# The last five batches' norms go into the rounds, the loop of rounds is written out, and idle products stand ahead of the first transposes

## What is computed

```
xn = layernorm(x)                       # (x - mean) / sqrt(var + eps), no weights
s  = mamba(xn)                          # W_in, causal convolution, silu, delta, scan over the tokens, W_out
g  = silu(ffn(xn))                      # (silu(xn wg) * (xn wu)) wd
x  = x + s * g
```

## Time and profile before

| what | value |
|---|---|
| median of 3 runs | 764.2 us (763.67 to 766.95) |
| the profiled execution: own time, span | 764.31 us, 762.5 us |
| busy: TensorE, VectorE, ScalarE, GpSimd | 660.6, 651.2, 495.9, 492.1 us |
| scans, line 1678 | 128 instructions, 288.5 us |
| first scan starts | 334.20 us |
| mean granted TensorE clock | 0.974 |

### The profile page before, as it was taken

One profiled execution on the slowest core, in us unless ns is written; L12 is line 12 of the kernel. 1 busy time (PEld: TensorE's weight loads), 2 busy tenths in 40 slices (PEclk: granted clock), 3 DMA queues, 4 the chain that ended last, 5 costly groups with the idle time before them and its releaser, 6 DMA issues. The chain is left out here.

```text
span 762.5 us, 13530 instructions
## 1 busy us (share of the span) xinstructions
PE 660.6 (87%) x3984; PEld 486.1 (64%) x3984; DVE 651.2 (85%) x1124; ACT 495.9 (65%) x1002; POOL 492.1 (65%) x306
## 2 busy tenths in 40 slices
PE   0898999999899964779998998998998999988785
PEld 0875556556555542347776886777787777767665
DVE  4968877777566646899999999899999999999998
ACT  0565666666444434778779778677787787797453
POOL 1002663000054545058899999999999999999995
PEclk9999999999999995989999999999999999999999
DMA  7900110001222218525515535335237156065000
GB/s 176 313 1 11 39 38 24 0 0 28 62 71 67 64 49 101 152 84 166 138 48 150 123 100 125 98 112 138 68 112 179 31 157 161 17 176 129 1 13 16
DMA packets 43223, 67.48 MB, mean 88 GB/s; under 512 B 6297, under 2 KB 30369, under 8 KB 43169
## 3 DMA queue, kind: packets, MB, share of 16 engines
q1 hardware_dynamic: 31888, 48.42, 20.7%
q0 software_dynamic: 9552, 17.85, 11.5%
q10 hardware_dynamic: 1728, 0.57, 0.5%
HBM read 46.08 MB, written 9.74 MB: 73 GB/s over the span
## 5 line engine op out<-in xcount | busy, mean ns | idle before, releaser
L1678 DVE TENSOR_TENSOR_SCAN xnT_all<-psum,nfT_all 128x1024 f32<-128x1024 f32 x128 | 288.5, 2277 | 0.0
L1258 PEld LDWEIGHTS psum<-W_out,xnT_all 128*128 128x128 f32 x2048 | 235.7, 192 | 60.2 <-issue 37.9
L1258 PE MATMUL psum<-W_out,xnT_all 128*128 128x128 f32 x2048 | 241.7, 276 | 31.6 <-DVE acc L1694 29.4
L1423 ACT ACTIVATE psum<-delta,A 128x511 f32<-128x511 f32 x256 | 165.0, 682 | 72.5 <-DVE xnT_all L1678 72.4
L1238 POOL TENSOR_TENSOR nfT_all<-nf_rows,du 128x1024 f32<-128x1024 f32 x63 | 147.2, 2361 | 30.9 <-DVE nfT_all L1760 29.8
L1238 POOL TENSOR_TENSOR nfT_all<-attn_all,du 128x1024 f32<-128x1024 f32 x64 | 157.5, 2605 | 0.0
L570 POOL DMA_INDIRECT moe_dram<-xnT_all x40 | 38.8, 969 | 121.1 <-ACT xnT_all L826 121.1
L1694 DVE SCALAR_TENSOR_TENSOR acc<-psum,Cc,acc 128x128 f32<-128x128 f32 x284 | 78.2, 340 | 6.2 <-PE psum L1258 6.0
L559 POOL DMA_INDIRECT xs_dram<-nf_rows,pos x32 | 33.6, 1050 | 74.7 <-DVE pos L880 55.8
L1258 PE MATMUL psum<-vo_all,W_taps 128*128 (+4 forms) x128 | 60.2, 618 | 3.0 <-DVE vo_all L1790 2.3
L1460 ACT ACTIVATE ts<-psum,Cc 128x128 f32<-128x128 f32 x188 | 52.8, 360 | 4.1 <-PE psum L1258 4.1
(11 more groups left out here) (215 smaller groups left out, 1111.6 us busy)
## 6 DMA issues: line engine op xcount, KB each, us to landing
nf_rows<-bt_dram SPq DMA_DIRECT2D x32, 512.0 KB, 4.7
attn_all<-bt_dram SPq DMA_DIRECT2D x32, 512.0 KB, 4.1
delta<-rl POOLq DMA_DIRECT2D x7, 512.0 KB, 6.9
e<-ab POOLq DMA_DIRECT2D x7, 512.0 KB, 5.8
delta<-e POOLq DMA_DIRECT2D x7, 512.0 KB, 6.3
xs_dram<-attn_all SPq DMA_DIRECT2D x4, 645.0 KB, 8.6
xnT_all<-xs_dram SPq DMA_DIRECT2D x40, 64.5 KB
x_all<-in_x_dram SPq DMA_DIRECT2D x8, 256.0 KB, 6.0
```

Of the source, the lines that this page charges most:

```text
L1258: return nc.tensor.matmul(o, l, r, start=start, stop=stop)
L1423: ins = nc.scalar.activation(dA[:, i % RA, k, 1:L], delta[:, p, h, 1:L], ACT.Exp, scale=A[:, h, 2 * q + k:2 * q + k + 1])
L1678: nc.vector.tensor_tensor_scan(hring[:, i % R, :, :].rearrange("p n l -> p (n l)"), dA[:, i % RA, :, :].rearrange("p n l -> p (n l)"), dbx ...
```

## The change

- `KEEP_WARM = 13` products (`ident` with 512 columns of `xn1T_all`, into bank 3, which nothing reads) stand on TensorE ahead of `turn(0)`. They wait for nothing.
- Batches 3 to 7 are no longer normed by VectorE. `shifts(2)` makes their reciprocals and `nb1 = -mean * reciprocal`, and ScalarE norms batch b + 3 in round b at q = 4 (`norm_later`, four activations with scale and bias by row) into a buffer of its own, `xnb`. TensorE turns it at q = 5, behind `ffn_down` (`turn_later`, into bank 4), ScalarE copies it out behind `gate_tanh` (`turned_later`), and TensorE waits for that copy at q = 6, before `x_in(b + 2, 0)`. This happens in rounds 0 to 4.
- `turn(3)` to `turn(7)` and `turned(3)` to `turned(7)` go from the first preparation. TensorE's wait before round 0 is for `F["xT"]` at 2 in place of 7.
- The copy of batch 1's turned norm (VectorE) stands behind `residual(6)`, not behind `residual(7)` and `moments(2)`.
- An Exp of one column (`touch`) stands on ScalarE behind `ssm_out` of the first preparation.
- In round 0 both `conv_gate` stand behind the first scan.
- The loop over rounds 1 to 4 is written out on every engine.

```diff
+            KEEP_WARM = 13
...
+            xnb = sb6("xnb", [P, TPB, D])
+            nb1 = sb6("nb1", [P, NT])
+            LATER = 3
+
             def xn1(i):
-                if i < 4:
-                    return ts[:, i, :, :]
-                return hff[:, i - 4, :].rearrange("p (j d) -> p j d", d=D) if i < 7 else ow[:, :, :]
+                return ts[:, i, :, :] if i < LATER else xnb[:, :, :]
...
-                with eng.Fori(0, (NB - 4) // 2) as r:
-                    round_(r * 2 + 1, 1, scan=True, prep=True, ahead=True, end=True)
-                    round_(r * 2 + 2, 0, scan=True, prep=True, ahead=True, end=True)
-                round_(NB - 3, 1, scan=True, prep=True, ahead=True, end=True)
+                for b in range(1, NB - 2):
+                    round_(b, b % 2, scan=True, prep=True, ahead=True, end=True)
...
                         x_in(b + 2, 1)
-                        turn(3)
-                        turn(4)
-                        turn(5)
-                        turn(6)
-                        turn(7)
...
                     if scan and prep and not end:
-                        pe.wait_ge(F["xT"], NB - 1)
+                        pe.wait_ge(F["xT"], 2)
...
                             elif q == 5:
                                 ffn_down()
+                                if b + LATER < NB:
+                                    turn_later(b + LATER)
+                        if q == 6 and b + LATER < NB:
+                            pe.wait_ge(F["xT"], b + LATER)
                         if q >= 6 and ahead:
...
+                def turn_later(i):
+                    pe.wait_ge(S["hf"], at(i - LATER, "hf", KF))
+                    pe.wait_ge(F["xn"], i + 1)
+                    for j in range(TPB):
+                        ins = nc.tensor.transpose(bank[bM[0]][:, j * P:(j + 1) * P], xn1(i)[:, j, :], ident)
+                    ins.then_inc(F["xT_ps"], 1)
...
+                for _ in range(KEEP_WARM):
+                    mm(bank[3], ident, xn1T_all[:, 0:L])
                 turn(0)
...
+                def norm_later(i):
+                    act.wait_ge(F["rs"], len(GROUPS) + 1)
+                    if i > LATER:
+                        act.wait_ge(F["xT_ps"], i)
+                    for j in range(TPB):
+                        k = i * TPB + j
+                        ins = nc.scalar.activation(xn1(i)[:, j, :], x_all[:, k, :], ACT.Identity,
+                                                   bias=nb1[:, k:k + 1], scale=rs1[:, k:k + 1])
+                    ins.then_inc(F["xn"], 1)
+
+                def turned_later(i):
+                    act.wait_ge(F["xT_ps"], i + 1)
+                    nc.scalar.activation(xn1T_all[:, i * L:(i + 1) * L], bank[bM[0]], ACT.Copy).then_inc(F["xT"], 1)
...
                         ssm_out()
+                        nc.scalar.activation(touch[:, :], eps[:, :], ACT.Exp)
                         abs_relu(0)
...
-                        turned(3)
                         conv_silu(b + 2, 0)
-                        turned(4)
                         conv_silu(b + 2, 1)
-                        turned(5)
-                        turned(6)
-                        turned(7)
...
+                        if scan and q == 4 and b + LATER < NB:
+                            norm_later(b + LATER)
                         if scan and q == 5:
                             gate_tanh()
+                            if b + LATER < NB:
+                                turned_later(b + LATER)
...
+                def shifts(g):
+                    c = slice(GROUPS[g][0] * TPB, (GROUPS[g][-1] + 1) * TPB)
+                    dve.wait_ge(F["std"], g + 1)
+                    nc.vector.reciprocal(rs1[:, c], std1[:, c]).then_inc(F["rs"], 1)
+                    dve.wait_ge(F["rs"], g + 1)
+                    nc.vector.scalar_tensor_tensor(nb1[:, c], mean1[:, c], -1.0, rs1[:, c], ALU.mult, ALU.mult)\
+                        .then_inc(F["rs"], 1)
...
                         residual(6)
+                        dve.wait_ge(F["xT_ps"], 2)
+                        nc.vector.tensor_copy(xn1T_all[:, L:2 * L], bank[Gb[1]]).then_inc(F["xT1"], 1)
                         residual(7)
                         moments(2)
-                        dve.wait_ge(F["xT_ps"], 2)
-                        nc.vector.tensor_copy(xn1T_all[:, L:2 * L], bank[Gb[1]]).then_inc(F["xT1"], 1)
...
                         deltas()
-                        norms(2)
+                        shifts(2)
                         drives()
...
-                        if q == 0 and not end:
-                            conv_gate(0)
-                            conv_gate(1)
                         if q == 0 and prep and end:
                             conv_gate(0)
                         scans(q, (0,))
-                        if q == 0 and prep and end:
+                        if q == 0 and prep:
+                            if not end:
+                                conv_gate(0)
                             conv_gate(1)
```

## The result

| | before | changed |
|---|---|---|
| median (20 runs each) | 763.92 us | 757.38 us |
| profiled execution: own time, span | 764.31, 762.5 us | 758.20, 756.3 us |
| busy TensorE, VectorE, ScalarE, GpSimd | 660.6, 651.2, 495.9, 492.1 | 670.0, 646.4, 502.3, 491.8 |
| mean granted TensorE clock | 0.974 | 0.981 |

The ratio is 0.9927, with a 95% interval of 0.9911 to 0.9942: 5.6 us gained (4.4 to 6.8), where the medians are 6.5 apart and the profiled executions 6.1. The forecast was 757.5.

The account below looks back on a forecast made before the run. VectorE, busy 51.2 of 53.2 us a round, was taken to bound the kernel. Start -5.5, loop -2.0 and turn +0.7 sum to -6.8 from 764.31, giving 757.5 us; range 753.5 to 762.

Parts of the forecast that it names:

- 3.05 us put down up to `softplus_high`: Between the layers: `softplus_high` starts 3.05 us earlier, by 2.1 from TensorE's clock and 1.0 from Exp's table load.
- Norms off VectorE ahead of the first scan, and the slow start of round 0: Norms save 4.8 us and gates 1.2 before the first scan; TensorE's slow `ssm` then makes VectorE wait 1.8.
- The loop: Rounds 1 to 4: writing them out removes VectorE's 2.97 us stall at the jump back, -2.0 us net.
- Exp's table: First preparation: the 1.28 us table load moves from the chain to behind `ssm_out`, gaining 1.0 us.
- The clock at `x_in`: `x_in` of batch 0: idle products hold TensorE's clock up, gaining 2.1 us, between nothing and 3.4.
- The first rival: Ahead of the first transposes the clock falls in the gap; nothing gained at `x_in`, -4.8 us, 759.5; chance 0.14.
- The bound of 3.4 us: First transposes and `x_in` of batch 0: 3.4 us is the most that a clock held up gives back.
- The cap by the loads: Residual of batch 7 needs the last load, so ScalarE's list can come forward by 3.0 us and no more.
- The turn in the rounds: Rounds 0 to 4: four transposes behind `ffn_down` cost 0.15 us a round, +0.7 in all (0 to +3.0).
- -5.5 at the start: From layer 0's end into round 0: 9.05 us gained at the first scan, 5.5 left (-3.5 to -8.0).
- ScalarE's insert: In five rounds ScalarE's norms and copy go on the path, +11.5 us with TensorE's part; 768.3, chance 0.06.

Follow-up runs that it names:

- e7: Changed kernel with sixteen idle products and the norm tiles of batches 3 to 7 made again by VectorE ahead of the first scan; 758.60 us, ratio 0.9954.
- e6: Changed kernel with sixteen idle products and both `conv_gate` of round 0 ahead of the first scan again; 755.58 us, ratio 0.9913.
- e8: Changed kernel with sixteen idle products and six more ahead of `ssm` of batch 1 in round 0; 754.40 us, ratio 0.99.
- e11: Changed kernel with sixteen idle products, two more ahead of `ssm` of batch 0 and six ahead of `ssm` of batch 1; 752.29 us, ratio 0.9859.
- e4: Kernel before with only the loop over rounds 1 to 4 written out; 760.11 us, ratio 0.9982.
- e2: Changed kernel with no idle products (`KEEP_WARM = 0`); 756.77 us, ratio 0.9927.
- e1: The changed kernel itself, run again beside its variants on one chip; 757.07 us, ratio 0.9935 to the kernel before.
- e9: The changed kernel itself, run again on a third chip; 756.15 us, ratio 0.9928 to the kernel before.
- e3: Changed kernel with sixteen idle products in place of thirteen; 756.65 us, ratio 0.9929.
- e10: Changed kernel with sixteen idle products and the turn's four transposes made three times each in rounds 0 to 4; 759.96 us, ratio 0.997.

## Why the prediction was right, step by step

The time came out at 757.38 for 757.5, and most steps as they were put down. But part of the nearness is luck. One term was too large by some 2 us. Against the 3.05 us put down up to `softplus_high` only 1.21 came, 1.84 too little, and of that 0.7 came back at the turn, 0.56 by layer 0's earlier end, 0.25 at round 0 and 0.05 at the loop; 0.32 went the other way at the end. So the span fell by 6.20 where 6.8 was put down. And the median with which the forecast agrees to 0.1 us lies between two kinds of execution, near 756 and near 759.4.

- **Norms off VectorE ahead of the first scan, and the slow start of round 0.** Put down: 6.0 us of earlier scan (norms and gates), of which 2.45 are left at round 1, with VectorE waiting 1.8 for TensorE at the lower clock. Measured: 64.34 against 67.04, so 2.70, with a wait of 1.56. e7 shows that most of the norms' length is paid (4.46 of 5.14), e6 that the first scan's start counts for little, and e8 that the loss is TensorE's clock: 1.81 us of it come back when the clock is held. This step is shown by the stretches of the traces; of the times only e11 against the changed kernel is clear of the noise.
- **The loop.** Put down -2.0; measured -2.05 in the trace, and alone in e4 1.4 us (0.2 to 2.5) by time and rounds of 53.08 in the trace. The two branches by the Trainium skill ("Advanced Engine Details and Errata", "Control Flow Timing"), 0.3 us, do not cover it. That the 2.97 us belong to the jump is shown; whether code is fetched in them is open (e4).
- **Exp's table.** Put down 1.0; 1.16 between the two profiled executions. Right.
- **The clock at `x_in`: mis-sized.** I took 2.1 us, "nearer to the upper end". From `x_in`'s start to `ssm`'s end it was 15.39 us before and 15.34 in the changed kernel's profiled execution: 0.05. `softplus_high` came 1.21 nearer to the transposes and not 3.05, and the Exp accounts for 1.16 of that. On average over executions thirteen products give nothing measured (e2 against e1, 756.8 and 757.1). The first rival, that the clock falls in the gap and nothing is gained at `x_in`, was right as to the profiled execution and e1's; in e9 the clock outlasted the gap and fell 1.0 us later, and `x_in` gained nothing there either. The reason that I gave for the higher value (a part at full clock in any case) held for the kernel before just as well, and its `x_in`, 10.01 us here, was 8.74 without any product in e4. The bound of 3.4 us left out `ssm` of batch 0, whose clock also turned out to vary (1.91 to 3.60 us). The cap by the loads was the wrong one: with a clock at full 2.25 us arrive, less than the 3.0 it allowed, and it is VectorE's own list that stops the rest (e3).
- **The turn in the rounds: mis-sized.** Put down +0.7, measured 0.00 in rounds of 53.08. I had allowed 0.15 us a round (0.45 less the 0.23 idle would have been 0.22); TensorE now starts the projection 3.12 us behind the start of `ffn_down` where it was 3.07, and VectorE's wait is still 0.62. e10 shows that all beyond would have been paid.
- **Not in the prediction.** The first transposes came 0.56 us earlier in the profiled execution; layer 0 had ended earlier, and no part of the change touches it. Behind round 5's second gate 0.32 us were lost, with a new wait of 0.23 for TensorE early in round 7 (at 709.22); e4, with the written-out loop alone, has it too (0.22), e10 has not, and its cause is open.

So -5.5 at the start was -4.47, of which -0.56 is not the change's; -2.0 was -2.05; +0.7 was 0; and +0.32 was not foreseen. Of the rivals on the other side, ScalarE's insert is out by its waits (1.16 us left behind the norms); how much more it would bear was not tried.

## What to carry to other kernels

Work that keeps the clock up is worth something only if it reaches right up to the work that is to profit, at every gap of the chain: thirteen products that ended 2.6 to 3.2 us ahead gave nothing at `x_in` in three traces, sixteen that reached up to it shortened the chain but not measurably the median, and sixteen with eight more in the two later gaps (e11) took 3.9 us off the changed kernel and made the times even. When a chain is cut ahead of a stage, read which engine the stage waits for next before counting the whole cut; here 4.25 us of the first scan's start were worth 0.5. An insert into a nearly gapless engine was free about up to the idle time ahead of the next instruction that another engine waits for, and was paid almost in full beyond.

## What the runs showed of the hardware

- The hardware loop's jump back held VectorE for 2.97 us, net 2.05 us for two passes, with two transfers of an instruction queue around the start of the stall. Text written out twice as long showed no stall in its place.
- The executions of the changed kernel divide by TensorE's clock: 756.0 us at a mean clock of 0.986 or more, 759.4 at 0.982 or less.
- The length of a gap did not decide alone whether the clock fell. It held through 3.20 us ahead of `ssm` of batch 0 in e3 and had fallen by the end of the same 3.20 us in e8; it held through 2.19 us there in e2 and e9 and fell at the end of 2.19 us in the changed kernel. It held through 1.06 and 1.58 us (e8 and e11, ahead of `ssm` of batch 1).
- Four 128x128 activations with scale and bias from SBUF took 1.65 us, four that scale out of PSUM 1.12.
